# Routing the tokens to experts in two parts, with a fixed region of rows per expert, and the output norm's statistics taken batch by batch

## The chip, the core and the metric

The kernel runs on one core of a Trainium2 chip. The metric is the time of one execution on the device in microseconds, as the median of several executions. TensorE (PE) multiplies and turns matrices, VectorE (DVE) and ScalarE (ACT) work on elements, GpSimd (POOL, here Pool) does elementwise work and issues the indirect transfers, SyncE (SP) issues plain transfers. The engines run side by side and wait for one another through semaphores.

## What is computed

One layer on x of 16 batches x 128 positions x 128 features, in float32. First an attention over each batch, with 16 heads of 64, shared keys and values, one extra null key, a position bias and a causal mask; then a layer norm of its output y; then a mixture of experts on y, whose result is added to x:

```python
def ln(x, g): ...                       # layer norm over the 128 features, gain g, no offset
y = ln(attention(x, ...) @ Wout, g_out)
shared_out = expert(y, sg, su, sd)      # expert: (silu(y @ g.T) * (y @ u.T)) @ d.T, 352 wide
probs = softmax(y @ wr.T + rb)          # 7 routed experts
scores, idx = top_k(probs, 2)
scores = scores / scores.sum(-1)
out = shared_out + sum_e w[e] * expert(y, rg[e], ru[e], rd[e])    # w: the two scores, 0 elsewhere
return x + out
```

Only the two chosen experts need be computed for a token, so the kernel sends each token's y to two of them.

## The kernel before

*Attention.* run_steps runs 19 steps t on every engine (16 batches, three stages deep): in step t TensorE makes the queries of batch t, the scores of batch t - 1, turns P and mixes the values of batch t - 2, and makes the output product of batch t - 3 (project, 16 + 2 matmuls as the trace counts them). Each engine's step is an order written out by hand. VectorE takes each output into y_sb (keep_y). Steps 17 and 18 have only the last batches in them. For batches 0 to 11 the norm of y is spread over these steps: centre_y(0) and scale_y(0) in step 17 on VectorE, with ScalarE's square_y(0) between, gain_y(0) in step 18. Batches 12 to 15 follow after the last step, the same way.

*Routing.* TensorE turns y (12 batches, then 4), ScalarE copies it to YT, and TensorE multiplies by the router's weights; the logits of all 16 batches come together (logits_made). VectorE adds the bias and picks two experts by a chain of small instructions in which each waits for the one before (own). TensorE counts by two products with a strict triangle and a matrix of ones how many rows of each batch go to each expert (ranks_made). VectorE sums these over the batches (run_up), rounds each expert's count up to tiles of 128 rows, sums the tiles (tiles_up) and from them gets each row's place (row_index) in sent_rows, a table in DRAM, in which the experts' tiles lie one behind the other. It then writes the shares, and the table of which expert each of 38 tiles belongs to (tile_expert).

*Tiles.* run_tiles runs 16 shared tiles (one per batch, from YT) and 38 routed ones through a pipeline of four steps: gate and up products (12 matmuls with GH, GL in two precisions), Silu and product, turn, down product. TensorE and VectorE enter it after the table. Pool meanwhile issues 32 indirect transfers, one per batch and choice, each sending 128 rows (y, share, destination) to their places (L485). When all have landed SyncE loads the tiles of rows into a ring of four (L348), each new one when an older is free. The unused rows were filled beforehand by one transfer (L344). Each routed tile's result goes out by an indirect transfer (L491), and at the end all results are loaded and added.

The lines of the profile that recur: L1079 is TensorE's matmul and L1076 its transpose, both in helpers, so tiles tell them apart. L887 and L891 are the scores on VectorE, L623 the exponentials on ScalarE, L761 and L764 the statistics of x, L780 the scaling of x, L732 to L738 the chain of the inverse square root, L864 the gain.

## Time and profile before

| what | us |
|---|---|
| median of 3 runs | 449.41 (448.5 to 451.06) |
| the profiled execution | 449.6 |
| its span in the trace | 447.9 |
| PE busy | 354.8 |
| DVE busy | 285.0 |
| ACT busy | 278.1 |
| POOL busy | 229.6 |

All times in the text are in microseconds from the start of the span. Between the span and the execution's time lie 1.7 us. A busy share is an average over stages: up to some 268 us the attention runs, up to 294 the routing, up to 324 the shared tiles, from 337 to 432 the routed tiles, and the rest adds the results. An idle time in brackets at the end of a row is that of the engine just before the instruction, with the instruction that ended it. A row of a stretch begins with its bounds and length; then come the busy time and the instructions (x) of PE, PE's weight loads, DVE, ACT and POOL, or of DVE alone, then the clock granted to TensorE as a share of 2.4 GHz, the busy share of the DMA engines and GB/s.

### The profile page before, as it was taken

What the parts mean: (1) busy time and instruction counts of PE and PEld (TensorE: products, weight loads), DVE (VectorE), ACT (ScalarE), POOL (GpSimd) and SP (SyncE); (2) the same over time, 40 slices, a digit from 0 to 9 for tenths busy, and PEclk for the clock granted to TensorE, in tenths of its full rate; (3) what the DMA queues carried; (4) which work ended last, traced back from release to release, by engine and by line L of the source; (5) the groups of instructions that cost most, each with busy time, mean ns of one, the idle gap of its engine ahead of it and who ended that gap; (6) DMA issues with size and microseconds to landing.
All of it is one profiled execution on the core that took longest, in us unless ns stands there. A gap on an engine that the chain in (4) does not pass through costs nothing.

```text
span 447.9 us, 10071 instructions
## 1 busy us (share of the span) xinstructions
PE 354.8 (79%) x2917; PEld 296.4 (66%) x2918; DVE 285.0 (64%) x1075; ACT 278.1 (62%) x931; POOL 229.6 (51%) x250
## 2 busy tenths in 40 slices
PE   0286574999999999999999877279908999999940
PEld 0275464677777777777777556279908899998930
DVE  2849246778888888878788886655503555555524
ACT  1384455999999999999999852325503444444410
POOL 5025723777777777777775613067760344444430
PEclk9998886999999999999999996569976999999995
DMA  5716390000000000000000000011111211112108
GB/s 161 243 55 192 106 218 0 2 2 1 1 2 1 3 1 1 3 1 1 2 1 3 2 1 0 0 36 56 51 51 41 56 54 52 48 59 59 41 18 271
DMA packets 29190, 21.28 MB, mean 48 GB/s; under 512 B 4288, under 2 KB 26842, under 8 KB 29150
## 3 DMA queue, kind: packets, MB, share of 16 engines
q1 hardware_dynamic: 23392, 14.23, 12.2%
q0 software_dynamic: 2240, 4.23, 2.7%
q10 hardware_dynamic: 3518, 2.33, 1.8%
q8 instruction: 20, 0.33, 0.3%
q14 instruction: 20, 0.16, 0.1%
HBM read 12.95 MB, written 8.21 MB: 47 GB/s over the span
## 4 chain that ended last, share of the span: by engine, by line
PE 71%; DVE 12%; ACT 6%; DMA 4%; issue 4%; POOL 2%; ACTq 0%; POOLq 0%; DVEq 0%
PE bank L1079 54%; PE bank L1076 16%; POOL sent_rows L485 2%; ACT p_space L623 2%; DMA q_space<-in_L_cond_g_dram 1%; DMA xnT<-result_rows 1%; DVE p_space L887 1%; ACT xn L550 1%; DVE p_space L761 1%; DVE low L891 1%; DVE xn L864 1%; DMA sent_rows<-biasm_space,row_index 1%; DVE stat L738 1%; ACT pT L642 0%; DMA result_rows<-oT_space,dest_ring 0%
## 5 line engine op out<-in xcount | busy, mean ns | idle before, releaser
L454 POOL TENSOR_TENSOR p_space<-p_space,inv 128x516 f32<-128x516 f32 x64 | 66.9, 1046 | 66.5 <-DVE inv L899 66.5
L623 ACT ACTIVATE p_space<-p_space,low 128x129 f32<-128x129 f32 x256 | 98.9, 391 | 1.1 <-DVE low L891 1.1
L887 DVE SCALAR_TENSOR_TENSOR p_space<-bank,rn,biasm_space 128x129 f32<-128x129 f32 x256 | 72.1, 344 | 22.4 <-PE bank L1079 22.2
L445 POOL TENSOR_TENSOR biasm_space<-bias,madd 128x516 f32<-128x516 f32 x64 | 75.4, 1189 | 8.1 <-DVE p_space L887 8.0
L491 POOL DMA_INDIRECT result_rows<-oT_space,dest_ring x38 | 37.3, 983 | 62.3 <-DVE dest_ring L1059 62.3
L696 ACT ACTIVATE biasm_space<-bank 128x384 f32<-128x384 f32 x54 | 26.6, 492 | 56.4 <-PE bank L1076 56.4
L623 ACT ACTIVATION_READ_ACCUMULATOR p_space<-p_space,low 128x1 f32 x256 | 48.3, 189 | 0.0
L1079 PE MATMUL bank<-GH,yh 128*128 (+1 forms) x108 | 41.2, 381 | 7.5 <-DVE yl L1030 7.5
L1079 PE MATMUL bank<-DT,biasm_space 128*128 (+1 forms) x324 | 45.7, 278 | 1.3 <-ACT biasm_space L696 1.3
L1076 PE MATMUL bank<-ident,p_space 128*128 128x128 f32 (+1 forms) x272 | 45.8, 285 | 0.4 <-ACT pT L642 0.4
L891 DVE TENSOR_REDUCE low<-p_space 128x4 f32<-128x516 f32 x64 | 44.2, 691 | 2.2
L1079 PEld LDWEIGHTS bank<-DT,biasm_space 128*128 128x128 f32 x324 | 43.5, 194 | 1.8 <-issue 1.8
L1079 PEld LDWEIGHTS bank<-KB,q_space 64*128 64x128 f32 x512 | 33.6, 194 | 14.6 <-issue 9.2
L1079 PE MATMUL bank<-pT,V 128*64 128x256 f32 x256 | 41.6, 404 | 1.7 <-ACT pT L642 1.3
L1079 PE MATMUL bank<-KB,q_space 64*128 64x129 f32 x512 | 42.9, 298 | 0.0
L642 ACT ACTIVATE pT<-bank 128x512 f32<-128x512 f32 x64 | 37.1, 582 | 6.4 <-PE bank L1079 6.3
L1079 PE MATMUL bank<-xnT,wq_sb 128*128 128x128 f32 x256 | 37.1, 291 | 1.2 <-ACT sq L614 1.2
L1079 PEld LDWEIGHTS bank<-xnT,wq_sb 128*128 128x128 f32 x256 | 32.8, 200 | 6.7 <-issue 5.0
L1030 DVE TENSOR_TENSOR yl<-bank,yh 128x128 fp32r<-128x128 f32 x38 | 11.1, 292 | 40.7 <-ACT yh L707 40.7
L1079 PE MATMUL bank<-GL,yh 128*128 (+1 forms) x108 | 36.2, 335 | 0.0
L1079 PE MATMUL bank<-GH,yl 128*128 (+1 forms) x108 | 36.1, 334 | 0.0
L1076 PE MATMUL bank<-ident,q_space 128*128 128x128 f32 x40 | 12.0, 301 | 30.0 <-DMA q_space<-sent_rows 13.1
(209 smaller groups left out, 708.7 us busy)
## 6 DMA issues: line engine op xcount, KB each, us to landing
sent_rows<-fill_row SPq DMA_DIRECT2D x1, 2470.0 KB, 14.5
q_space<-sent_rows SPq DMA_DIRECT2D x38, 65.0 KB, 1.9
xs<-in_x_dram SPq DMA_DIRECT2D x4, 256.0 KB, 7.0
bias<-bias_rows SPq DMA_DIRECT2D x1, 1024.0 KB, 5.8
xn<-result_rows SPq DMA_DIRECT2D x4, 256.0 KB, 5.2
xnT<-result_rows ACTq DMA_DIRECT2D x4, 256.0 KB, 5.9
out_dram<-xs SPq DMA_DIRECT2D x4, 256.0 KB, 2.4
o_space<-in_L_ffn_rd_dram SPq DMA_DIRECT2D x5, 176.0 KB, 3.0
```

The costliest lines, as they stand in the source:

```text
L445: nc.gpsimd.tensor_tensor(biasm[:, b % 2, heads, :], bias[:, heads, :], madd[:, b:b + 1, :].to_broadcast([P, HC, KEYS]), ALU.add).then_inc ...
L454: nc.gpsimd.tensor_tensor(v, v, spread(inv[:, b % 2, heads], KEYS), ALU.mult).then_inc(p_normed, 1)
L485: nc.gpsimd.indirect_dma_start(out=sent_dram[:, :], out_offset=bass.IndirectOffsetOnAxis(ap=row_index[:, k, b:b + 1], axis=0), in_=send[k] ...
L491: nc.gpsimd.indirect_dma_start(out=result_dram[:, :], out_offset=bass.IndirectOffsetOnAxis(ap=dest_ring[:, m:m + 1], axis=0), in_=result[: ...
L623: last = nc.scalar.activation(v, v, ACT.Exp, bias=low[:, b % 2, h:h + 1], accum_out=den[:, b % 2, h:h + 1])
L642: nc.scalar.activation(pT[:, c % 2, :], bank[turned_bank(t, c)][:, :], ACT.Copy).then_inc(p_kept, 1)
L696: nc.scalar.activation(hT[:, (m - 3) % 2, :], bank[4 + (m - 3) % 2][0:IC, 0:ICH * P], ACT.Copy).then_inc(hT_kept, 1)
L887: last = nc.vector.scalar_tensor_tensor(Pb[:, q, h, :], src, rn[:, q, h:h + 1], biasm[:, q, h, :], ALU.mult, ALU.add)
L891: nc.vector.tensor_reduce(low[:, q, c * HC:(c + 1) * HC], Pb[:, q, c * HC:(c + 1) * HC, :], AX_X, ALU.max, negate=True).then_inc(maxed, 1)
L1030: nc.vector.tensor_tensor(yl[:, m % 2, :], src, yh[:, m % 2, :].bitcast(F32), ALU.subtract).then_inc(yl_made, 1)
L1076: return nc.tensor.transpose(out, in_, ident[0:n, 0:n])
L1079: return nc.tensor.matmul(out, a, b, start=start, stop=stop, skip_group_check=True)
```

## The change

Every expert gets a fixed region of 2,048 rows in sent_rows, so that a row's place needs its expert's number, the count of earlier rows and nothing of the other experts (eoff is added to the first totals). The table grows to 118 tiles, its filling is split over four transfers. Because regions are not adjacent, SyncE reads each tile's first row from a new table, tile_row, four numbers at a time (find_rows). With places independent of later batches, routing runs in two parts: PARTS is batches 0 to 11 and 12 to 15. Part 0 has its logits, choice and count before and around the last output product, its ranks, marks and shares and its 24 sends after; part 1 follows with 8 sends; the table comes last. The send buffers lie elsewhere, part 0's in bias and madd. The norm takes its statistics with bn_stats on each output (keep_y) and bn_aggr; the passes of VectorE over the whole tile and ScalarE's squares go. The constants for counting are made by Pool in step 4. Pool no longer waits for down_kept between the sends.

```diff
+    PARTS = (range(0, Y_FIRST), range(Y_FIRST, NB))
...
+    REGION = NB * S
+    SENT = NE * NB + ROUTED - TOP * NB
+    FILLS = 4
...
+        sent_dram = nc.dram_tensor("sent_rows", (SENT * P, ROW), F32, kind="Internal").ap()
...
+        send = ((rows_in_tile(bias, Y_FIRST), rows_in_tile(madd, Y_FIRST)),
+                (shared(p_space, 0, NB - Y_FIRST, ROW), shared(p_space, (NB - Y_FIRST) * ROW, NB - Y_FIRST, ROW)))
...
-            sp.dma_start(sent_dram.rearrange("(t p) c -> p t c", p=P),
-                         fill_row[:, :].unsqueeze(1).to_broadcast([P, ROUTED, ROW])).then_inc(rows_filled, 16)
-
...
+            for k in range(FILLS):
+                tiles = range(k * SENT // FILLS, (k + 1) * SENT // FILLS)
+                sp.dma_start(sent_dram[tiles.start * P:tiles.stop * P, :].rearrange("(t p) c -> p t c", p=P),
+                             fill_row[:, :].unsqueeze(1).to_broadcast([P, len(tiles), ROW])).then_inc(rows_filled, 16)
...
+            def find_rows(r, n):
+                sp.load(row_regs[0:n], tile_row[0:1, bass.ds(r, n)])
+                return [sp.snap(reg, min_val=0, max_val=(SENT - 1) * P) for reg in row_regs[0:n]]
...
+            sp.wait_ge(table_made, 1)
             sp.wait_ge(rows_sent, 16 * TOP * NB)
...
+            found = find_rows(0, RING)
+            for m in range(RING):
+                load_rows(found[m], m)
...
+                found = find_rows(RING * i + RING, RING)
...
-                    load_rows(RING * i + (RING + m), m)
+                    load_rows(found[m], m)
...
+                if t == 4:
+                    pool.wait_ge(expert_turned, 3 * E)
+                    nc.gpsimd.memset(ones[:, :], 1.0).then_inc(sort_consts, 1)
+                    for k in range(len(PARTS)):
+                        nc.gpsimd.memset(run_up[k][:, :, :, :], 0.0).then_inc(sort_consts, 1)
...
 
...
-                    need(pool, down_kept, min((k * NB + b - 6) // 2, NB - 3))
...
+            pool.wait_ge(rows_filled, 16 * FILLS)
+            for k, batches in enumerate(PARTS):
+                pool.wait_ge(row_index_made, k + 1)
+                for n in range(TOP):
+                    pool.wait_ge(send_made[k][n], 3)
+                    for b in batches:
+                        nc.gpsimd.indirect_dma_start(
+                            out=sent_dram[:, :], out_offset=bass.IndirectOffsetOnAxis(ap=row_index[:, n, b:b + 1], axis=0),
+                            in_=send[k][n][:, b - batches.start, :], in_offset=None).then_inc(rows_sent, 16)
...
-            def square_y(k):
-                b = slice(0, Y_FIRST) if k == 0 else slice(Y_FIRST, NB)
-                act.wait_ge(y_centred, k + 1)
-                nc.scalar.activation(y_squares[:, b, :], y_sb[:, b, :], ACT.Square).then_inc(y_squared, 1)
...
+                if t == NB + 2:
+                    keep_yT(2)
...
-                if t == NB + 1:
-                    square_y(0)
...
+                if t == NB + 1:
+                    keep_yT(0)
+                    keep_yT(1)
...
+            nc.scalar.activation(send[0][1][:, :, 0:D], y_sb[:, 0:Y_FIRST, :], ACT.Copy).then_inc(send_made[0][1], 1)
+            weigh(0)
+            keep_yT(Y_FIRST // 4)
+            for m in range(TOP):
+                nc.scalar.activation(send[1][m][:, :, 0:D], y_sb[:, Y_FIRST:NB, :], ACT.Copy).then_inc(send_made[1][m], 1)
...
+            def scale_y(g):
+                for b in range(4 * g, 4 * g + 4):
+                    last = nc.vector.tensor_scalar(y_sb[:, b, :], y_sb[:, b, :], y_mv[:, b, 0:1], ra[:, b:b + 1], ALU.subtract, ALU.mult)
+                last.then_inc(y_scaled, 1)
+
+            def gain_y(g):
+                dve.wait_ge(y_scaled, g + 1)
+                b = slice(4 * g, 4 * g + 4)
...
+            def norm_y(k):
...
                 dve.wait_ge(y_kept, b.stop)
-                own(nc.vector.tensor_reduce(ma[:, b], y_sb[:, b, :], AX_X, ALU.add))
-                own(nc.vector.tensor_scalar(ma[:, b], ma[:, b], 1.0 / D, None, ALU.mult))
...
-                own(nc.vector.tensor_reduce(va[:, b], y_squares[:, b, :], AX_X, ALU.add))
...
+                for n in PARTS[k]:
+                    last = nc.vector.bn_aggr(y_mv[:, n, :], y_bst[:, n, :])
+                own(last)
+                own(nc.vector.tensor_scalar(va[:, b], y_mv[:, b, 1], EPS, None, ALU.add))
                 own(rsqrt(ra[:, b], va[:, b], ta[:, b], own))
...
+                for g in groups:
+                    scale_y(g)
+                    if g > groups.start:
+                        gain_y(g - 1)
+                gain_y(groups.stop - 1)
...
+            def choose(k):
...
+                dve.wait_ge(logits_made, k + 1)
...
+                nc.vector.tensor_tensor(load[:, b, :], chosen[:, 0, b, :], chosen[:, 1, b, :], ALU.add).then_inc(load_made, 1)
+                nc.vector.tensor_tensor(share[:, 3, b], best[:, 1, b], best[:, 0, b], ALU.subtract).then_inc(gap_made, 1)
...
+            def rank(k):
...
+                base = eoff[:, :] if k == 0 else run_up[0][:, 0, PADS[0] + Y_FIRST - 1, :]
+                nc.vector.tensor_copy(totals[:, b, :], tot)
+                nc.vector.tensor_tensor(up[:, 0, pad, :], tot[:, 0, :], base, ALU.add)
...
+                side, far = 0, 1
...
+                own(nc.vector.tensor_tensor(place[:, b, :], place[:, b, :], up[:, side, pad:pad + n, :], ALU.add))
+                for m in range(TOP):
+                    last = nc.vector.tensor_tensor(placed[:, m, b, :], chosen[:, m, b, :], place[:, b, :], ALU.mult)
...
+                nc.vector.tensor_copy(row_index[:, :, b], row_of[:, :, b]).then_inc(row_index_made, 1)
...
@@ -906,7 +1010,8 @@
                 def keep_y():
                     if on(3):
                         dve.wait_ge(y_made, t - 2)
-                        nc.vector.tensor_copy(y_sb[:, t - 3, :], bank[7][:, 0:D]).then_inc(y_kept, 1)
+                        nc.vector.tensor_copy(y_sb[:, t - 3, :], bank[7][:, 0:D])
+                        nc.vector.bn_stats(y_bst[:, t - 3, :], bank[7][:, 0:D]).then_inc(y_kept, 1)
...
-                if t == NB + 1:
-                    centre_y(0)
...
+                if t == NB + 1:
+                    dve.wait_ge(router_turned, 1)
+                    nc.vector.tensor_copy(router_wT[:, 0:NE], bank[3][:, 0:NE]).then_inc(router_kept, 1)
+                    norm_y(0)
+                if t == NB + 2:
+                    choose(0)
                 keep_y()
...
-                if t == NB + 1:
-                    scale_y(0)
-                if t == NB + 2:
-                    gain_y(0)
...
-            centre_y(1)
-            scale_y(1)
-            gain_y(1)
...
+            for k in range(len(PARTS)):
+                if k > 0:
+                    norm_y(k)
+                    choose(k)
+                mark(k)
+                side = rank(k)
+                share_out(k)
+
+            own(nc.vector.scalar_tensor_tensor(tiles_int[:, 0, :], run_up[1][:, side, PADS[1] + NB - Y_FIRST - 1, :], float(P - 1), eoff[:, :],
+                                               ALU.add, ALU.subtract))
             own(nc.vector.tensor_scalar(tiles_int[:, 1, :], tiles_int[:, 0, :], P.bit_length() - 1, None, ALU.logical_shift_right))
-            nc.vector.tensor_copy(tiles_of[:, :], tiles_int[:, 1, :])
+            nc.vector.tensor_scalar(skipped[:, :], tiles_int[:, 1, :], -float(P), float(REGION), ALU.mult, ALU.add)
...
+            own(nc.vector.tensor_tensor(passed_on[:, :, :], passed[:, :, :],
+                                        skipped[:, 0:NE - 1].unsqueeze(1).to_broadcast([P, ROUTED, NE - 1]), ALU.mult))
+            own(nc.vector.tensor_reduce(tile_skip[:, :], passed_on[:, :, :], AX_X, ALU.add))
+            nc.vector.tensor_scalar(tile_expert[:, RING:RING + ROUTED], tile_float[:, :], 1.0, None, ALU.add)
+            nc.vector.scalar_tensor_tensor(tile_row[:, :], iota_tile[:, :], float(P), tile_skip[:, :], ALU.mult, ALU.add).then_inc(table_made, 1)
...
+            def turn_y(g):
+                pe.wait_ge(y_normed, g + 1)
...
+                pe.wait_ge(p_kept, NCH * (NB - 1) + max(1, g + 1))
+                for b in range(4 * g, 4 * g + 4):
+                    last = turn(bank[y_bank[g]][:, (b % 4) * P:(b % 4 + 1) * P], y_sb[:, b, :])
...
+                if t == NB + 1:
+                    pe.wait_ge(biased, NCH * NB)
+                    turn(bank[3][:, 0:NE], router_sb[:, :]).then_inc(router_turned, 1)
+                if t == NB + 2:
+                    logits(2)
...
+                if t == NB + 1:
+                    turn_y(0)
+                    turn_y(1)
                 mix(2, 2)
+                if t == NB + 1:
+                    turn_y(2)
+                    logits(0)
+                    logits(1)
...
-            for batches in (range(Y_FIRST), range(Y_FIRST, NB)):
-                pe.wait_ge(y_normed, 1 if batches.start == 0 else 2)
-                for b in batches:
-                    last = turn(bank[b // 4][:, (b % 4) * P:(b % 4 + 1) * P], y_sb[:, b, :])
...
+            pe.wait_ge(oT_kept, 2 * NB)
+            count(0)
+            turn_y(3)
+            logits(3)
+            count(1)
...
+                    pe.wait_ge(table_made, 1)
...
-            pe.wait_ge(table_made, 1)
```

TensorE at the end of the attention, from the third-last output product on; `p_space` is P, `pT,V` the mix, `wo_sb` the output product, `xn` is y, `xnT` its turned copy. Before:

```order
L1079 MATMUL bank<-wo_sb,oT_space 128x128 x8
L1079 MATMUL bank<-null_out,pnT 128x128
L1076 MATMUL bank<-ident,p_space 128x128 x4
L1079 MATMUL bank<-pT,V 64x256 x4
L1076 MATMUL bank<-ident,p_space 128x128 x4
L1076 MATMUL bank<-ident,p_space 16x128
L1079 MATMUL bank<-pT,V 64x256 x4
L1079 MATMUL bank<-wo_sb,oT_space 128x128 x8
L1079 MATMUL bank<-null_out,pnT 128x128
L1076 MATMUL bank<-ident,router_sb 128x7
L1076 MATMUL bank<-ident,xn 128x128 x12
L1079 MATMUL bank<-router_wT,xnT 128x7 x12
```

The same engine after, from the last turn of P's null column to the counting (`o_space` holds the load):

```order
L1139 MATMUL bank<-ident,p_space 16x128
L1139 MATMUL bank<-ident,xn 128x128 x8
L1142 MATMUL bank<-pT,V 64x256 x2
L1139 MATMUL bank<-ident,xn 128x128 x4
L1142 MATMUL bank<-router_wT,xnT 128x7 x8
L1142 MATMUL bank<-pT,V 64x256 x2
L1142 MATMUL bank<-router_wT,xnT 128x7 x4
L1142 MATMUL bank<-wo_sb,oT_space 128x128 x8
L1142 MATMUL bank<-null_out,pnT 128x128
L1142 MATMUL bank<-o_space 128x84 x2
L1139 MATMUL bank<-ident,xn 128x128 x4
L1142 MATMUL bank<-router_wT,xnT 128x7 x4
```

The turns of y for batches 0 to 11 and their logits moved ahead of the last output product, among the last two mixes; the count of part 0 moved ahead of the turns of part 1.

VectorE in step 17, from the last exponentials' reciprocals on. Before (centring, then ScalarE's squares, then scaling; `xn` is y, `xnT` the squares):

```order
L850 TENSOR_REDUCE stat<-xn 128x12
L851 TENSOR_SCALAR stat<-stat 128x12
L852 TENSOR_TENSOR xn<-xn,stat 128x1536
L899 RECIPROCAL inv<-den 128x4
L909 COPY xn<-bank 128x128
L857 TENSOR_REDUCE stat<-xnT 128x12
L858 TENSOR_SCALAR stat<-stat 128x12
```

VectorE after, from behind the square root's chain of part 0 to the first instructions of the choice:

```order
L889 TENSOR_SCALAR xn<-xn,stat 128x128 x8
L895 TENSOR_TENSOR xn<-xn,gor 128x512
L889 TENSOR_SCALAR xn<-xn,stat 128x128 x4
L895 TENSOR_TENSOR xn<-xn,gor 128x512 x2
L1013 COPY xn<-bank 128x128
L1014 BN_STATS stat<-bank 128x6
L917 TENSOR_TENSOR o_space<-bank,rbr 128x84
L921 TENSOR_REDUCE best<-o_space 128x12
```

The centring no longer stands ahead of the reciprocal; the whole norm stands behind it and ahead of the copy of batch 14's output, and the choice of part 0 stands ahead of the copy of batch 15's.

## Rows read from the trace of the kernel before

**Rows 1.** TensorE in order of time: start, duration, instructions, idle before with releaser.

```profile
75.57 1.91 PE L1079 MATMUL bank<-xnT,wq_sb 128*128 128x128 f32 x8
...
260.49 0.65 PE L1079 MATMUL bank<-pT,V 128*64 128x256 f32 x4
...
265.68 2.05 PE L1079 MATMUL bank<-wo_sb,oT_space 128*128 128x128 f32 x16 [0.69 <-ACT oT_space L654]
...
277.83 1.11 PE L1076 MATMUL bank<-ident,xn 128*128 128x128 f32 x4 [0.82 <-DVE xn L864]
279.72 1.85 PE L1079 MATMUL bank<-router_wT,xnT 128*128 128x7 f32 x8 [0.78 <-ACT xnT L684]
...
294.32 0.63 PE L1079 MATMUL bank<-GH,yh 128*128 128x352 f32 x1 [7.49 <-DVE yl L1030]
...
323.82 0.49 PE L1076 MATMUL bank<-ident,biasm_space 128*128 128x128 f32 x3
337.43 0.48 PE L1076 MATMUL bank<-ident,q_space 128*128 128x128 f32 x1 [13.12 <-DMA q_space<-sent_rows]
...
344.22 0.27 PE L1076 MATMUL bank<-ident,q_space 128*128 128x128 f32 x1
...
357.94 0.32 PE L1076 MATMUL bank<-ident,q_space 128*128 128x128 f32 x1 [0.53 <-issue]
```

**Rows 2.** Pool in order of time: the first and the last of 32 sends.

```profile
293.72 1.21 POOL L485 DMA_INDIRECT sent_rows<-p_space,row_index  x1 [13.92 <-DVE p_space L1011]
...
333.20 0.96 POOL L485 DMA_INDIRECT sent_rows<-biasm_space,row_index  x1 [0.30 <-issue]
```

**Rows 3.** Chain of waits, behind the last send: start, duration, what.

```profile
333.20 2.31 DMA sent_rows<-biasm_space,row_index
335.53 1.86 DMA q_space<-sent_rows
```

**Rows 4.** Stretches of 2 us: all engines, granted clock, DMA.

```profile
268.00:270.00 2.00, 0.16 (x3) 0.01 (x1) 1.75 (x2) 0.00 (x0) 1.32 (x4) 1.00 0.00 0
272.00:274.00 2.00, 2.00 (x12) 2.00 (x11) 0.70 (x2) 1.16 (x3) 0.00 (x0) 0.50 0.00 0
298.00:300.00 2.00, 2.00 (x14) 2.00 (x13) 0.90 (x3) 1.04 (x3) 1.68 (x2) 0.83 0.20 67
```

**Rows 5.** ScalarE in order of time: the end of the last exponential of batch 15.

```profile
258.81 0.19 ACT L623 ACTIVATION_READ_ACCUMULATOR p_space<-p_space,low 128x1 f32 x1
```

**Rows 6.** VectorE in order of time: statistics, scaling, scores, gain.

```profile
14.45 0.38 DVE L764 BATCH_NORM_AGGREGATE p_space<-p_space 128x2 f32<-128x6 f32 x4
...
21.96 2.14 DVE L780 TENSOR_SCALAR xn<-xs,p_space,stat 128x128 f32<-128x128 f32 x8
...
59.99 1.13 DVE L887 SCALAR_TENSOR_TENSOR p_space<-bank,rn,biasm_space 128x129 f32<-128x129 f32 x4 [3.38 <-PE bank L1079]
...
217.05 1.13 DVE L887 SCALAR_TENSOR_TENSOR p_space<-bank,rn,biasm_space 128x129 f32<-128x129 f32 x4 [0.85 <-PE bank L1079]
...
277.08 0.69 DVE L864 TENSOR_TENSOR xn<-xn,gor 128x512 f32<-128x512 f32 x1
```

**Rows 7.** VectorE by stretch: square root, choice, ranks, tiles, places, table.

```profile
263.88:266.15 2.27, 1.89 (x11) 1.00 0.00 0
281.60:285.60 4.00, 3.58 (x14) 0.50 0.00 0
286.92:289.27 2.35, 2.11 (x8) 0.50 0.00 0
289.27:290.77 1.50, 1.26 (x9) 0.50 0.00 0
290.77:292.17 1.40, 1.30 (x6) 0.50 0.00 0
292.74:293.90 1.16, 1.06 (x7) 0.50 0.00 0
```

**Rows 8.** DMA issues of the page: KB of one, us from issue to landing.

```profile
sent_rows<-fill_row SPq DMA_DIRECT2D x1, 2470.0 KB, 14.5
```

230 lines of the change are left out of this document (110 added, 120 removed).

## Prediction, made before the changed kernel was run

> **What bounds the kernel now.** I read the chain of waits first. It runs through TensorE for the attention (to 268 us), then through VectorE's routing, then TensorE's 16 shared tiles, then Pool's sends, then TensorE's 38 routed tiles. Three places in [rows 1] matter. TensorE starts the first shared tile at 294.32, 26 us after the last attention product; it ends the turning steps of the shared tiles at 323.82 + 0.49 = 324.3; and it then stands 13.12 us until 337.43 for the first routed rows. [rows 2] shows who fills those 13 us: Pool issues 32 sends, the first at 293.72, the last at 333.20, 39.5 us in all or 1.27 each, and they can start only when every row has its place. [rows 3] gives the rest: the last send lands 2.31 us after its start, the row load takes 1.86. So the sends bound the start of the routed tiles, the shared tiles hide 30 us of them. [rows 4] shows what idling costs: TensorE is granted full clock at 268 to 270, half (1.2 GHz) at 272 to 274 after it had stood nearly 2 us, and climbs again between 298 and 300. The reader should see two things: the wait is 13.1 us, and ending it takes either earlier sends or nothing.
>
> **The change, part by part.** Of the 32 sends 24 belong to batches 0 to 11. They now start when part 0 is ranked, not when all is. But the shared tiles start only after part 1's routing and the table, since VectorE runs all of it first. So two dates decide: the first send, and the first shared tile. I follow VectorE and TensorE through the tail.
>
> *Norm of part 0.* VectorE takes it after the last reciprocal of batch 15, which waits for the last exponential, at 258.81 + 0.19 = 259.0 [rows 5]. With the router's copy it starts at 259.3. 12 aggregates at 0.38/4 [rows 6] are 1.1. The chained links cost 2.27/11 = 0.206 each [rows 7], 12 of them 2.5: 262.9. A scale of one batch is 2.14/8, some 0.26 [rows 6]; 8 are 2.0: 264.9; a gain of four batches 0.7, or 0.6 back to back [rows 6]: 265.6 for group 0, 267.2 for group 1, 267.8 for group 2. The whole-tile passes and ScalarE's squares that this replaces cost nothing now on the path but VectorE's own turn.
>
> *TensorE's tail.* Its order is now: turn groups 0 and 1, mix, turn group 2, logits of groups 0 and 1, mix, logits of group 2, and only then the output product of batch 15, which stood at 265.68 before [rows 1]. It idles from 262.5 to 265.6, waiting for group 0; before, an idle of 2 us took the clock away [rows 4], so I take the half level from there. At that level four turns are 1.1 and four batches of logits 1.85 [rows 1]. The output product is 18 matmuls, and 8 of the same shape took 1.91 at half clock [rows 1], so 4.2 (2.5 at full, from the 2.05 and the row after it). A mix is 0.65 at full [rows 1], I take 1.2. Sum: 265.6 + 1.1 = 266.7; group 1 267.2 to 268.3; mix 269.5; turn 270.6; two logits 274.3; mix 275.5; logits 277.3; output product 281.5. So the last attention output comes 13 us later than before. VectorE does choose(0) meanwhile: the 13 links of 112 elements took 4.0 with the gap [rows 7], and between those and the 0.206 of 16 elements I take 3.5 for 84: 280.8, hidden. Count(0) follows the output product, 1.3 (from 285.60, the end of one window of [rows 7], to 286.92, the start of another): 282.9. Rank(0) is the 2.35 plus 1.40 of [rows 7], less one link and smaller: 3.2, so 286.1. Sharing out was the 0.6 between two windows there: 286.8.
>
> *Sends.* Before, the share ended at 292.7 [rows 7] and the first send started at 293.72 [rows 2], 1.0 later. Now 287.8, and 39.5 on, 327.3, the last, if none waits for part 1 (its indices are there at 302, its first send is due at 318). Landed 329.6, loaded 331.5 [rows 3]. The removed waits on down_kept cost nothing: the spacing was 1.27 with them.
>
> *Part 1.* Four aggregates 0.4, 12 links 2.4, 4 scales 1.0, a gain 0.7: 4.6, to 291.4. Turn, copy and logits took 281.60 - 277.70 = 3.9 before (277.83 in [rows 1], the start of choosing in [rows 7]): 295.3. Choosing on 28 elements 2.8: 298.1. Count 1.3: 299.4. Rank with two doublings less, 2.1: 301.5. Sharing 0.6: 302.1. The table was 1.50 + 0.85 [rows 7]; one link goes, a 228-element multiply and reduction come, and the row of each tile: 3.3, 305.4. From the table's end (293.6) to the first shared tile (294.32) it was 0.7: **306.2**, 11.9 later than before.
>
> *Shared tiles and after.* They run 30 us as before, with the same half-clock start: 324.3 + 11.9 = 336.2. The rows are there at 331.5, 4.7 earlier. TensorE goes on at once, 1.2 before 337.43. The two first routed steps took 344.22 - 337.43 = 6.8 at half clock; from 344.22 to 357.94 six took 13.72, or 2.29 each [rows 1]. At full clock 4.6, plus a tenth for the register load that the wait used to hide: 4.7, gain 2.1. Together 3.3.
>
> *What costs nothing.* bn_stats of each output is 0.2 on VectorE, which stands 0.85 before its next group [rows 6]; TensorE is the bound there. Pool's five constants move into step 4, behind its last norm of P, where it next waits for a reciprocal that TensorE's and ScalarE's pace sets; I take nothing, and uncovered they delay one turn of P once, by no more than two sends' length, 2 us. The fill grows from 38 to 118 tiles, 14.5 [rows 8] to about 45 us, from 54 to 100, and nothing waits for it until 287; VectorE's score group took 1.13 inside the old fill and 1.13 long after it [rows 6]. SyncE's register load per four tiles lies in front of waits, with four tiles (9 us) of lead. Its price is not in the trace; TensorE's own costs under 0.8, in the 0.53 of idle at 357.94 [rows 1]. Zero to 0.8, once, and I take zero.
>
> Sum: 449.6 (the profiled execution, 0.2 above the median of three) - 3.3 = **446.3**.
>
> **Rivals.** *The clock holds.* If it falls late or not at all in the tail, the turns, mixes, logits and output product lose about half of their 16 us: choose(0) begins at 272.5, not 277.3, part 1 saves 2 more, the shared tiles start 7 earlier and their slow start (2 us) goes. Then the sends bind: 327.3 - 5 + 4.2 = 326.5, and the time is 446.3 - 9 = 437. For it: the rows hold one fall only, and after it the output product's place is a guess of mine by one idle. Against: that idle was nearly 2 us, this one is 3 and a second of 0.5 follows. In parts, 438 to 443.5. Chance 0.20.
>
> *A longer chain.* I count some forty hand-overs between engines at their best; 3 to 5 us more in them gives 449 to 451.5, level with before. Chance 0.08.
>
> *Slower: sends stretched by VectorE.* 14 sends now fall in 287.8 to 305.4, where VectorE works without pause, not beside tiles. The first old send, which overlapped the table, took 1.21, against 0.96 for the last [rows 2]. At 0.25 more for each of the 14, the last is 3.5 later, under the 4.7 of slack: no change. It decides from 0.34 a send, and the kernel is slower by over 0.5% from (4.7 + 5.6)/14 = 0.74 a send; at 1.0 a send 455.6. Chance 0.06. The Trainium skill (SBUF — State Buffer, "Who interferes with whom") has the rule behind this: copies, casts and tensor_scalar of VectorE in a two-port mode shut GpSimd out of the port that its descriptors are written through. By the page's 3100 ns in place of 620 for a covered send, 14 of them would cost 35 us and, 4.7 of it slack, the time would be about 477; VectorE's instructions of those kinds here are short, some 3 us in all, and no row above shows such a send.
>
> *Slower: the fill.* 30 us of extra writing lie beside steps in which TensorE is never idle; if it slowed them by a fifth, 6 us, the time is 452. Nothing in [rows 6] shows it. Chance 0.05.
>
> **How the numbers follow.** Forecast 0.61, its own range 443.8 to 449; about two thirds of it lie below 447.2, the 0.5% under which a measurement of this kernel can't tell a gain from none. Faster 0.42 + 0.20 = 0.62; same 0.19 + 0.08 = 0.27; slower 0.11. The range takes in the partly held clock and the longer chain: 440.5 to 450.5.
>
> **What would show it.** In the profile after: the output product of batch 15 near 277 with the clock at half (held clock: before 273 at full); the first send near 288, 24 sends without a gap; the first shared tile near 306; no wait between shared and routed tiles, at full clock; row loads waiting for nothing. Wrong would be a gap before the first routed tile (the sends still bind), sends above 1.5 us apart, or attention steps longer than before between 68 and 100 us.

## The result, and the profile after

| | median us | runs | ratio to before, 95% interval |
|---|---|---|---|
| before | 449.63 | 448.50 to 451.06 | |
| after | 446.02 | 444.06 to 447.13 | 0.9911 [0.9884, 0.9937] |

The change makes the kernel 0.9% faster by the ratio, 3.6 us (0.8%) by the medians. The profiled execution took 444.37 (span 442.5), which is 5.2 less than the profiled one of before and 1.7 below the median of after. That difference matters below.

TensorE in order of time, from the last attention steps to the first routed tiles (start, duration, instruction; in brackets the idle time before it and what ended it):

```profile
261.85 0.77 PE L1139 MATMUL bank<-ident,p_space 128*128 128x128 f32 x5
265.80 0.66 PE L1139 MATMUL bank<-ident,xn 128*128 128x128 f32 x4 [3.18 <-DVE xn L895]
267.43 1.11 PE L1139 MATMUL bank<-ident,xn 128*128 128x128 f32 x4 [0.97 <-DVE xn L895]
268.47 1.12 PE L1142 MATMUL bank<-pT,V 128*64 128x256 f32 x4
...
270.43 3.42 PE L1142 MATMUL bank<-router_wT,xnT 128*128 128x7 f32 x16
...
274.83 1.88 PE L1142 MATMUL bank<-router_wT,xnT 128*128 128x7 f32 x8
276.56 3.76 PE L1142 MATMUL bank<-wo_sb,oT_space 128*128 128x128 f32 x16
...
280.71 0.68 PE L1142 MATMUL bank<-o_space 128*128 128x84 f32 x4
289.88 1.12 PE L1139 MATMUL bank<-ident,xn 128*128 128x128 f32 x4 [8.49 <-DVE xn L895]
291.77 1.85 PE L1142 MATMUL bank<-router_wT,xnT 128*128 128x7 f32 x8 [0.78 <-ACT xnT L632]
296.54 1.05 PE L1142 MATMUL bank<-o_space 128*128 128x28 f32 x4 [2.92 <-DVE o_space L929]
304.35 0.63 PE L1142 MATMUL bank<-GH,yh 128*128 128x352 f32 x1 [6.75 <-DVE yl L1093]
...
333.93 0.30 PE L1139 MATMUL bank<-ident,q_space 128*128 128x128 f32 x1
...
338.17 0.27 PE L1139 MATMUL bank<-ident,q_space 128*128 128x128 f32 x1
```

Against [rows 1]: the first shared tile starts at 304.35 in place of 294.32, and the first routed tile at 333.93 in place of 337.43 and with no wait in front of it, where 13.12 stood. Pool in order of time, the first send, one in the middle and the last, against [rows 2]:

```profile
286.18 1.21 POOL L523 DMA_INDIRECT sent_rows<-bias,row_index  x1 [16.58 <-DVE bias L968]
...
304.17 1.07 POOL L523 DMA_INDIRECT sent_rows<-madd,row_index  x1 [0.30 <-issue]
...
325.73 0.96 POOL L523 DMA_INDIRECT sent_rows<-p_space,row_index  x1 [0.30 <-issue]
```

The sends start 7.5 sooner than before and end 7.5 sooner, in front of the last shared tiles. The chain that ended last holds more of VectorE (14%, 12% before) and no longer the sends (POOL had 2% of it); its line by engine on the page:

```profile
PE 72%; DVE 14%; ACT 6%; DMA 3%; issue 3%; ACTq 0%; POOLq 0%; DVEq 0%
```

In stretches of 20 us (busy time of PE, weight loads, DVE, ACT and POOL, then TensorE's granted clock, DMA share, GB/s):

```profile
260.00:280.00 20.00, 15.85 (x79) 12.64 (x79) 10.81 (x48) 5.46 (x9) 2.15 (x2) 0.67 0.00 1
280.00:300.00 20.00, 5.41 (x24) 4.31 (x23) 13.23 (x73) 3.73 (x8) 10.77 (x11) 0.59 0.10 34
300.00:320.00 20.00, 15.65 (x106) 15.66 (x107) 11.48 (x40) 7.50 (x21) 15.12 (x17) 0.81 0.16 55
320.00:340.00 20.00, 19.92 (x153) 19.71 (x152) 11.14 (x36) 10.61 (x30) 5.17 (x6) 1.00 0.14 40
```

In the profile before, these four stretches were granted 0.78, 0.53, 1.00 and 0.73. Both kernels run the end of the routing at half clock. Before, the clock fell a second time, under the 13.12 us wait, and was still at half (0.50 from 337 to 341) for the first routed tile. Now that second fall is gone, but the first one comes earlier and ends later: 0.50 from 268 to 280 and again from 284 to 304, where before it was 0.50 from 272 to 296. It lies on TensorE's own road to the shared tiles, which now holds the turns, the logits and the last output product one behind another.

Two rows of the same view of before, for the comparisons below, the 24 logits of batches 0 to 11 and the counting:

```profile
271.88 5.13 PE L1079 MATMUL bank<-router_wT,xnT 128*128 128x7 f32 x24
...
285.62 1.20 PE L1079 MATMUL bank<-o_space,q_space 128*128 128x112 f32 x4 [4.05 <-DVE o_space L971]
```

### The profile page after: what moved, and what is told of

It reads as the page before. It is cut to its first block, busy times and chain, and to the rows that moved or that the text cites. A ratio compares the mean times of both kernels' runs of the same rounds, so it can differ in the third digit from the quotient of the medians.

```text
span 442.5 us, 10208 instructions
## 1 busy us (share of the span) xinstructions
PE 355.2 (80%) x2921; PEld 295.9 (67%) x2922; DVE 289.0 (65%) x1148; ACT 276.7 (63%) x932; POOL 228.6 (52%) x252
## 4 chain that ended last, share of the span: by engine, by line
PE 72%; DVE 14%; ACT 6%; DMA 3%; issue 3%; ACTq 0%; POOLq 0%; DVEq 0%
PE bank L1142 56%; PE bank L1139 16%; ACT p_space L660 3%; DMA q_space<-in_L_cond_g_dram 2%; DMA xnT<-result_rows 1%; DVE p_space L991 1%; DVE xn L889 1%; ACT xn L588 1%; DVE p_space L806 1%; ACT pT L679 1%; DVE stat L781 1%; DVE low L995 1%; DVE stat L782 1%; DVE stat L783 0%; ACT q_space L642 0%
## 5 line engine op out<-in xcount | busy, mean ns | idle before, releaser
L1142 PE MATMUL bank<-GH,yh 128*128 (+1 forms) x108 | 40.2, 372 | 6.8 <-DVE yl L1093 6.8
L1142 PE MATMUL bank<-pT,V 128*64 128x256 f32 x256 | 42.5, 412 | 0.3 <-ACT oT_space L691 0.2
L1139 PEld LDWEIGHTS bank<-ident,p_space 128*128 128x128 f32 (+1 forms) x272 | 29.5, 140 | 9.3 <-issue 4.0
L1142 PE MATMUL bank<-wo_sb,oT_space 128*128 128x128 f32 x256 | 33.2, 285 | 1.2 <-DVE rn L783 0.7
```

The lines of the kernel that those rows point to most:

```text
L1139: return nc.tensor.transpose(out, in_, ident[0:n, 0:n])
L1142: return nc.tensor.matmul(out, a, b, start=start, stop=stop, skip_group_check=True)
```

## The experiments

Three dates tell nearly everything, so they stand in one table: the first send, the first shared tile, the first routed tile with the wait in front of it, then the rest of the span behind that. The column "at 237" is the start of one and the same output product of the attention, ahead of anything that the change moves. Each row is one profiled execution; the median is that of all timed runs of the kernel.

| kernel | at 237 | first send | first shared | first routed | wait | rest | median |
|---|---|---|---|---|---|---|---|
| before | 236.89 | 293.72 | 294.32 | 337.43 | 13.12 | 110.5 | 449.6 |
| after | 237.22 | 286.18 | 304.35 | 333.93 | none | 108.6 | 446.02 |
| after_again, the same kernel | 237.45 | 287.15 | 305.32 | 335.39 | none | 108.6 | 445.96 (one run) |
| e1 sends held | 237.71 | 301.17 | 304.42 | 345.59 | 11.40 | 110.2 | 457.7 (one run) |
| e2 norm alone | 237.07 | 289.56 | 290.15 | 333.29 | 12.66 | 109.6 | 445.29 |
| e6 split alone | 237.86 | 289.77 | 310.17 | 340.56 | none | 108.5 | 446.57 |
| e10, the same kernel | 236.54 | 287.39 | 307.80 | 337.73 | none | 108.8 | 448.39 (one run) |
| e3 after, early statistics | 237.79 | 285.12 | 303.29 | 332.86 | none | 108.6 | 443.38 |
| e4 after, clock held | 237.65 | 283.58 | 299.84 | 328.17 | 0.33 | 108.8 | 437.95 |
| e5 e3 and e4 | 237.05 | 279.84 | 296.12 | 324.51 | 0.41 | 108.9 | 435.53 |
| e9 after, clock held at the end | 236.32 | 285.99 | 304.27 | 332.55 | none | 108.8 | 443.60 |
| e7 norm alone, clock held | 237.57 | 288.72 | 289.31 | 332.42 | 15.13 | 110.1 | 445.03 |
| e8 split alone, clock held | 237.63 | 286.15 | 306.59 | 334.65 | none | 108.7 | 444.76 |
| e11 before, clock held | 236.50 | 294.33 | 294.93 | 337.99 | 15.10 | 110.3 | 451.20 |

The last part is 108.5 to 108.9 in every kernel that reaches the routed tiles without a long wait, and 109.6 to 110.5 in every one that waits 11 us or more there. So the span ends some 108.7 behind the first routed tile, and one or two later where the clock must first come back; the execution's time is about 1.8 more than the span. Everything below is about that date.

The column "at 237" says how far two traces can be compared. It differs by 1.5 over all rows, and by 1.3 between two executions of one kernel (e6 and e10), which already stand 2.4 apart at the attention's products near 46 us. A difference of about 1 us between the dates of two traces need not come from an edit.

**e1_hold: does the early start of the sends matter at all?** Pool waits for both parts' indices before the first send:

```diff
-                pool.wait_ge(row_index_made, k + 1)
+                pool.wait_ge(row_index_made, len(PARTS))
```

> The changed kernel with one wait moved: part 0's 24 sends also wait until part 1 is ranked (row_index_made 2), as the old kernel's did; regions, tables, fill and norm stay. Theory 1 (the earlier start of part 0's sends carries the gain): first send near 301 instead of 286.2, the last 39.5 later at 340.3, landed and loaded at 344.6, so TensorE stands 10.7 us before the first routed tile and loses its clock again; time 444.4 + 10.7 + 2.1 = 457. Theory 2 (the gain comes from the norm and from routed tiles that run better, the sends are hidden either way): time within 2 us of the changed kernel, 444 to 447.

Measured: 457.7. TensorE in order of time, the first routed tile:

```profile
345.59 0.48 PE L1139 MATMUL bank<-ident,q_space 128*128 128x128 f32 x1 [11.40 <-DMA q_space<-sent_rows]
```

With the sends 15.0 later the wait is back and the first routed tile comes 11.7 later. Within the changed kernel, the early sends are worth about 12 us on the first routed tile, 13 in the time of the profiled execution. That shows that the early start carries the gain, and says nothing yet of what it is worth against the kernel before.

**e2_before_bn: the other half, alone.** The kernel before, with the new norm, and with the gain of part 0 in step 17, where the changed kernel has it, in place of step 18:

```diff
-                        nc.vector.tensor_copy(y_sb[:, t - 3, :], bank[7][:, 0:D]).then_inc(y_kept, 1)
+                        nc.vector.tensor_copy(y_sb[:, t - 3, :], bank[7][:, 0:D])
+                        nc.vector.bn_stats(y_bst[:, t - 3, :], bank[7][:, 0:D]).then_inc(y_kept, 1)
...
-                dve.wait_ge(y_squared, k + 1)
-                own(nc.vector.tensor_reduce(va[:, b], y_squares[:, b, :], AX_X, ALU.add))
+                for n in range(b.start, b.stop):
+                    last = nc.vector.bn_aggr(y_mv[:, n, :], y_bst[:, n, :])
...
-                if t == NB + 2:
+                if t == NB + 1:
                     gain_y(0)
```

> The old kernel with the norm half of the change alone: bn_stats with each output copy, bn_aggr, scaling batch by batch, no passes over the whole tile and no squares on ScalarE; routing, sends and table as of old. The sends bound the old kernel, so each us by which the first send comes earlier is a us of gain. Theory 1 (the norm is worth little alone): part 1 of y is normed 3.8 us earlier, but TensorE's logits of batches 0 to 11 (5.1 us at half clock) then stand in front of it, so the first send is only 2 us earlier: 447.5. Theory 2 (the norm alone brings the whole gain and the split nothing on top of it): first send 4 us earlier, 445.5, level with the changed kernel.

Measured: 445.29, ratio 0.9905 [0.9873, 0.9937]. Theory 1 said 447.5; theory 2, 445.5, was right. The norm alone brings as much as the whole change. What the earlier gain of part 0 has in that was not run by itself. TensorE in order of time:

```profile
264.45 2.05 PE L1066 MATMUL bank<-wo_sb,oT_space 128*128 128x128 f32 x16 [0.69 <-ACT oT_space L650]
...
270.46 2.81 PE L1066 MATMUL bank<-router_wT,xnT 128*128 128x7 f32 x24
274.13 0.66 PE L1063 MATMUL bank<-ident,xn 128*128 128x128 f32 x4 [0.86 <-DVE xn L853]
...
290.15 0.63 PE L1066 MATMUL bank<-GH,yh 128*128 128x352 f32 x1 [7.48 <-DVE yl L1017]
```

Beside [rows 1]: the output product of batch 15 comes 1.2 earlier, since ScalarE has no squares (1.48, at 260.38 before) between its copies, and the turning of part 1, which waits for VectorE's norm, 3.7 earlier (274.13, not 277.83). The first send follows, 4.2 earlier, and the wait behind the shared tiles stays (12.66). The time fell by as much as the first send moved (4.3 and 4.2): in the kernel before, the norm in front of the first send stood on the road to the time. Here TensorE was at full clock for the 24 logits (2.81, not 5.13), but they weren't what the next turn waited for; e11 below shows the same from the other side.

**e6_split_oldnorm and e10_split_again: the split alone.** The changed kernel with the norm of before (centre_y, square_y, and scaling four batches at a time by tensor_tensor):

```diff
-                    last = nc.vector.bn_aggr(y_mv[:, n, :], y_bst[:, n, :])
...
+                dve.wait_ge(y_squared, k + 1)
+                own(nc.vector.tensor_reduce(va[:, b], y_squares[:, b, :], AX_X, ALU.add))
```

> The changed kernel (two parts, fixed regions, table of first rows) with the norm of the kernel before: VectorE sums and centres the rows, ScalarE squares them, VectorE sums the squares and scales four batches at a time. The missing fourth of the square: neither half, the norm alone (445.3), the split alone, both (446.0). Theory 1 (the split alone frees the sends' wait of 13 us but gives most of it back as a later first shared tile; I take the first send at 288 and the first shared tile at 308, four us later than in the changed kernel because part 1's norm is longer too): 448. Theory 2 (the two halves add, the norm is worth 4.3 and the split 0.7 less than nothing): 450.3. A rival reading of the square, that either half alone brings the same 4 us because both move the sends: 445.5.

> The split with the old norm once more, since its profiled execution was the longest of six (451.06, the others down to 445.1). Theory 1 (the first shared tile comes earlier, and the routed steps with it; 109 us follow the first routed step as in every trace here): a run of 445 to 447 with the first routed step at 335 to 337. Theory 2 (the difference lies behind the first routed step): the first routed step at 340.6 again.

Measured: 446.57 in six runs from 445.08 to 451.06, ratio 0.9902 [0.9883, 0.9921], and 448.39 in one more. The third expectation for e6, that either half brings the same four microseconds, is nearest by the median (445.5 against 448); the two traces lie nearer to Theory 1's dates of 288 and 308 (first send 287.39 and 289.77, first shared tile 307.80 and 310.17). The two traces part in front of the first routed tile, not behind it (108.8 and 108.5 follow): half as Theory 1 of e10 had it, though 337.73 is later than the 335 to 337 that I gave. This kernel scatters by 6 us, and only e3 by as much. The traces show from what the 2.4 between their first sends come: 1.3 is there at 237 us already (and still at the last turning of P, 263.96 and 262.64), and the rest is the clock's return. In e10 it came back within the last output product, whose 16 matmuls took 3.50 and the counting behind it 0.65; in e6 they took 3.76 and 1.15.

So the square without a held clock reads, in medians: neither 449.6, norm 445.3, split 446.6, both 446.0. The intervals of the three ratios (0.9905, 0.9902, 0.9911) cover one another. Each half is worth 3 to 4 us, and the second one nothing.

**e3_early: VectorE's chain.** The aggregates and the square root of part 0 go ahead of the last reciprocals of step 17:

```diff
+                if t == NB + 1:
+                    stats_y(0)
                 invert(3, 2)
```

> The changed kernel with part 0's aggregates and square root (3.5 us of VectorE) put ahead of the last reciprocal of step 17, where VectorE stood 2.3 us. Theory 1 (the tail is one chain from part 0's norm over TensorE to the first shared tile): y of group 0 is ready 2.3 us earlier, first shared tile near 302, time 442 against 444.4 of the profiled execution, ratio to the old kernel near 0.984. If the shorter idle of TensorE also keeps its clock, the output product takes 2.5 instead of 4.2 and the time is near 440. Theory 2 (the last reciprocal, 1.2 us later now, takes the gain back through Pool, the turn of P and the last mixes): no change, 446.

Measured: 443.38, ratio 0.9823 [0.9757, 0.9888], 2.6 off the changed kernel's median. The interval is wide because one of the four runs took 438.04, with the highest mean clock of the four (0.928), and the others 443.36 to 443.95; that run was not profiled. The expectation, 442 against the 444.4 of the profiled execution, was too much for the trace: it took 443.41, and all dates come 1.1 sooner. This execution was 0.6 later than the other at 237 us, so the edit itself gave some 1.7 of the 2.3. TensorE in order of time:

```profile
264.72 0.66 PE L1145 MATMUL bank<-ident,xn 128*128 128x128 f32 x4 [1.46 <-DVE xn L895]
266.35 1.11 PE L1145 MATMUL bank<-ident,xn 128*128 128x128 f32 x4 [0.97 <-DVE xn L895]
```

The idle in front of the first turn is 1.46 in place of 3.18, and the clock fell all the same.

**e4_warm: the clock.** TensorE computes products that nobody reads where it would wait: 3 in front of the first turn, 1 behind it, 10 behind the first count, then 1, 3 and 8, each of 384 columns (one of 256).

```diff
+            def warm(*widths):
+                for w in widths:
+                    mm(bank[4][:, P:P + w], ident[:, :], wq_sb[:, 0:w], True, True)
...
+                    pe.wait_ge(pn_kept, NB)
+                    warm(*[384, 384, 384])
                     turn_y(0)
+                    warm(*[384])
                     turn_y(1)
...
             count(0)
+            warm(*[384, 384, 384, 384, 384, 384, 384, 384, 384, 384])
```

> The changed kernel with products added that nothing reads (26 of 256 or 384 columns into a free PSUM bank), placed where TensorE waits between the last turn of P and the first shared tile, so that it never idles long. Theory 1 (half clock costs the tail some 5 us and the shared tiles' start 2): clock full from 260 to 330, choice of part 0 at 274 instead of 276.75, first shared tile near 299, last send near 322.5, first routed tile near 327, time 437.5. Theory 2 (the added products run past the waits and push the turns back, or the clock does not stay up): 444 to 450.

Measured: 437.95, ratio 0.9730 [0.9712, 0.9748], as Theory 1 had it. TensorE in order of time:

```profile
263.76 2.20 PE L1142 MATMUL bank<-wq_sb,ident 128*128 128x384 f32 x6 [0.73 <-ACT pnT L672]
266.21 0.66 PE L1139 MATMUL bank<-ident,xn 128*128 128x128 f32 x4 [0.24 <-DVE xn L895]
...
269.50 1.85 PE L1142 MATMUL bank<-router_wT,xnT 128*128 128x7 f32 x16
...
271.86 1.51 PE L1142 MATMUL bank<-router_wT,xnT 128*128 128x7 f32 x8
273.22 3.76 PE L1142 MATMUL bank<-wo_sb,oT_space 128*128 128x128 f32 x16
...
288.71 1.03 PE L1142 MATMUL bank<-router_wT,xnT 128*128 128x7 f32 x8 [0.34 <-ACT xnT L632]
...
299.84 0.40 PE L1142 MATMUL bank<-GH,yh 128*128 128x352 f32 x1 [1.31 <-DVE yl L1093]
...
328.17 0.33 PE L1139 MATMUL bank<-ident,q_space 128*128 128x128 f32 x1 [0.33 <-DMA q_space<-sent_rows]
```

The turns of part 0 take 0.66, where after has 1.11 from the second on, sixteen logits 1.85 in place of 3.42, the first shared tile comes 4.5 sooner and the shared tiles need 28.3 in place of 29.6. The last row shows that the sends now bind again, by a third of a microsecond: both roads to the first routed tile are about equally long. The clock was not held throughout: the output product of batch 15 ran at half here too (3.76).

**e9_warm_tail: which of these products counts.** Only the last eight are left:

```diff
             count(1)
+            warm(*[384, 384, 384, 384, 384, 384, 384, 384])
```

> The changed kernel with the last eight of the unread products alone, those behind part 1's counting, right ahead of the first shared tile. Nothing is left out. Theory 1 (they bring only the part of the gain that lies in the shared tiles themselves, which start at half clock: in the trace of the changed kernel the first shared tile to the first routed step takes 29.6, with all the products 28.3, and part of the 6.7 us wait may become busy work at half clock that ends a little late): 444.7 against 446.0. Theory 2 (the clock ahead of the shared tiles is what matters for all that follows, the routed steps too): 440.

Measured: 443.60 (443.24 to 444.15), ratio 0.9877 [0.9846, 0.9908]. In the trace the first shared tile stands where it stood (304.27) and the shared tiles take 28.3, 1.3 less, as Theory 1 had it. This execution was 0.9 earlier at 237 us and had the late clock of after_again below: from there to the first shared tile it took 67.95, after_again 67.87 and after 67.13, so the eight products moved nothing ahead of it. 2.4 against the median of after is more than that, but the two intervals overlap, and in after_again the shared tiles took 30.1, 1.8 more than with the added products. Theory 2 falls: the larger part of e4's gain, over 5 us, is made ahead of the shared tiles.

**e7_before_bn_warm and e8_split_oldnorm_warm: each half with the clock held.** Products like those of e4, in e2 (3, 1, 1, 6 and 11 of them) and in e6 (6, 1, 13, 1, 3, 8). The diff is two of the places in e7:

```diff
             turn(bank[4][:, 0:NE], router_sb[:, :]).then_inc(router_turned, 1)
+            warm(3)
...
             last.then_inc(logits_made, 1)
+            warm(6)
```

> The kernel before with the new norm alone (445.3 so far), and unread products in TensorE's waits: three behind the router's turning, one between the two parts, one ahead of the last logits, six behind them, eleven behind the counting. Nothing is left out. Against the changed kernel with such products (437.95) it shows what the split is worth once the clock is held. Theory 1 (here the sends end last and the products can only shorten the road to the first send, from 289.56 to some 287.5): 443, so the split is worth 5 us with a held clock and nothing without. Theory 2 (the gain from the products is a gain of clock alone, the same in both kernels): 437.5, and the split is worth nothing either way.

> The split with the old norm, and unread products in TensorE's waits (six ahead of part 0's turning, thirteen behind its counting, then one, three and eight). Nothing is left out. It shows what the norm is worth when the clock is held, against 437.95 with both halves. Theory 1 (with the clock held every us of VectorE's chain ahead of the table is on the path, twice: the norm of part 0 and that of part 1; from the two first sends, 289.8 against 286.2, and the longer norm of part 1): 442.5, the norm is worth 4.5. Theory 2 (the halves overlap here as they do without the products, 446.6 against 446.0): 438.5.

Measured: e7 445.03 (444.25 to 445.22), ratio 0.9893 [0.9876, 0.9909]; e8 444.76 (443.25 to 445.25), ratio 0.9888 [0.9852, 0.9923]. TensorE in e7 in order of time:

```profile
270.94 2.81 PE L1066 MATMUL bank<-router_wT,xnT 128*128 128x7 f32 x24
...
276.04 1.03 PE L1066 MATMUL bank<-router_wT,xnT 128*128 128x7 f32 x8
```

Its first routed tile, in the same view:

```profile
332.42 0.47 PE L1063 MATMUL bank<-ident,q_space 128*128 128x128 f32 x1 [15.13 <-DMA q_space<-sent_rows]
```

With the norm alone a held clock gives 0.3: it makes the wait for the sends longer (15.13) and little else. Theory 1 for e7 had the mechanism but 2 us too much for it. With both halves such products gave 8.1 (e4), with the split alone 1.8. Held, the square reads: norm alone 445.0, split alone 444.8, both 438.0. So the split is worth some 7 us on top of the norm once the clock is held, and nothing if it isn't. The norm's 6.8 on top of the split is an upper bound, since e8 carries two costs of its own. The six products ahead of the first turn ran past the date at which VectorE had group 0 ready (268.78), so the turn started at 270.89. And the clock was not held for part 1: its eight logits took 1.85, as at half clock, behind a wait of 2.30.

**e11_before_warm: the fourth corner.** The kernel before with the products of e7.

```diff
             last.then_inc(logits_made, 1)
+            warm(6)
```

> The kernel before with the same unread products (three behind the router's turning, one between the parts, one ahead of the last logits, six behind them, eleven behind the counting), neither half of the change. Nothing is left out. It is the last corner of the square with the clock held: norm alone 445.0, split alone 444.8, both 438.0. Theory 1 (in the kernel before every us ahead of the first send counts, and the products give back half a clock there: 24 logits in 2.8 instead of 5.1, four turnings and eight logits 1.3 sooner, the counting 0.5 sooner; 4.1 in all, of which the longer wait ahead of the first routed step takes 0.3): 446. Then in the kernel before most of what the norm alone brought (4.3) was clock, and the held-clock gains are 1, 1.2 and 8 us: the halves are worth their gain only together. Theory 2 (the products bring as little here as with the norm alone, 0.3): 449.6; the held-clock gains are 4.6, 4.8 and 11.6, near a plain sum.

Measured: 451.20 (449.73 to 452.70), ratio 1.0034 [1.0019, 1.0049]: slower, and both theories fall. TensorE in order of time:

```profile
271.30 2.81 PE L1079 MATMUL bank<-router_wT,xnT 128*128 128x7 f32 x24
273.98 1.04 PE L1079 MATMUL bank<-wq_sb,ident 128*128 128x384 f32 x2
277.25 1.11 PE L1076 MATMUL bank<-ident,xn 128*128 128x128 f32 x4 [2.23 <-DVE xn L864]
...
281.00 6.01 PE L1079 MATMUL bank<-wq_sb,ident 128*128 128x384 f32 x12
286.85 0.59 PE L1079 MATMUL bank<-o_space,q_space 128*128 128x112 f32 x4
```

The 24 logits are 2.3 faster and it helps nobody: the next turn waits for VectorE's old norm of part 1 until 277.25, and before it was 277.83 (in an execution that was 0.4 later at 237 us). Here VectorE sets the date, not the clock. Then the six products run at half clock, end at 287.0 instead of some 285, and the counting behind them starts at 286.85, where the same view of before has 285.62. With the 0.4 at 237 us the first send is 1.0 later than in before; the profiled execution (450.12) is one of the fastest of the ten, and what makes the median 1.5 higher than before's beyond this 1.0 is open. So this corner holds a cost of its own, and no sum over the square is drawn from it.

**e5_both: the best of them.** e3 and e4 in one kernel, with fewer products around the first turn than e4 has, against which this diff is:

```diff
-                    warm(*[384, 384, 384])
-                    turn_y(0)
                     warm(*[384])
+                    turn_y(0)
+                    warm(*[256])
                     turn_y(1)
```

> The changed kernel with both edits of the two runs before: the aggregates and the square root of part 0 are put ahead of the last reciprocals, and TensorE computes unread products (the identity by the query weights, into bank 4) where it would wait. Nothing is left out. Theory 1 (with the clock held the sends are what ends last, so an earlier date is worth what it moves the first send, and no more): the first send comes some 1.1 us before the 283.58 of the run with the products alone, and the time is 436.8. Theory 2 (the two edits add in full to the changed kernel's 446.0): 446.0 - 2.6 - 8.1 = 435.3.

Measured: 435.53 (435.04 to 435.75), ratio 0.9679 [0.9663, 0.9696], 3.2% faster than before and 2.4% faster than the change as made. The sum, 435.3, met the median and Theory 1, 436.8, did not. Theory 1 took the first send to move by 1.1; it moved by 3.7 between the two traces. The first turn of y stands 2.2 sooner (263.98, not 266.21): 0.6 of it is there at 237 us, the rest is the early statistics. Behind it the clock stayed full to the end of part 0:

```profile
269.62 1.06 PE L1148 MATMUL bank<-router_wT,xnT 128*128 128x7 f32 x8
270.53 2.03 PE L1148 MATMUL bank<-wo_sb,oT_space 128*128 128x128 f32 x16
```

where e4 needed 1.51 and 3.76 for the same. What it said of the end holds: the first routed tile moved as the first send did, 3.7 sooner both, and the profiled execution with them (435.34, not 438.96). By the medians it is 2.4, since the traced execution of e4 is the slowest of its four. That the sum met the median is therefore in part luck: it adds two gains, and in the trace a third thing, the clock behind the first turn, belongs to neither alone.

**after_again: a second trace of the changed kernel.**

> The changed kernel once more. Its runs lie in two groups, about 444.2 with a mean granted clock of 0.925 and about 446.4 with 0.908. Both theories expect one of the two; if it falls in the second, the trace shows in which stretch the clock is lower.

Measured: 445.96, with a mean granted clock of 0.906; the six runs of after have 0.925 twice (444.37 and 444.06) and 0.907 to 0.910 four times (445.88 to 447.13). TensorE in order of time:

```profile
276.79 3.76 PE L1142 MATMUL bank<-wo_sb,oT_space 128*128 128x128 f32 x16
...
281.20 1.15 PE L1142 MATMUL bank<-o_space 128*128 128x84 f32 x4
290.84 1.11 PE L1139 MATMUL bank<-ident,xn 128*128 128x128 f32 x4 [8.49 <-DVE xn L895]
...
305.32 0.63 PE L1142 MATMUL bank<-GH,yh 128*128 128x352 f32 x1 [6.77 <-DVE yl L1093]
```

In the first trace the clock was back at full when the counting ran (0.68); here it was not (1.15). The next turn is 0.96 later, the first shared tile 0.97, the first routed one 1.46 (335.39), the span 1.5. Of the 0.97 at the first shared tile 0.23 is there at 237 us already. The other 0.5 of the span lies in the shared tiles, 30.1 in place of 29.6. So the profiled execution lies below the median with a clock that came back in time for the counting; that the four runs of the lower clock are like after_again is read from their mean clock alone, since they weren't traced.

## Why the prediction was right, and where it wasn't

The forecast was 446.3 and the median is 446.02, inside the forecast's own range. The mechanism was right for the kernel with both parts; the credit that the prediction gave to each part was not. The steps, with what the profiled execution shows:

- **VectorE's norm of part 0** (start 259.3, group 0 normed at 265.6): 259.5 and 265.7. Links of 0.205 where I took 0.206. Right.
- **TensorE's tail at half clock**: right from the second turn on (1.11), the first still ran at full (0.66). Logits ended at 276.7, forecast 277.3; the output product at 280.8, forecast 281.5, since 16 matmuls took 3.76 and the last two 0.5. The prediction had placed all this by one idle of 3 us. The clock fell there in every trace of the split without added products, but behind idles of 3.2, of 4.3 (e6, e10) and of 1.46 (e3); in e2, with an idle of 2.1, it stayed full for the 24 logits behind it (2.81). So the length of the idle doesn't tell, and that the fall came where it was forecast is in part luck.
- **Counting part 0**, 1.3 from the output product's end to the first step of the ranks: the term that was mis-sized. It was 0.7 here (280.8 to 281.49), the counting's matmuls taking 0.68 because the clock had come back; 1.15 in the other trace. This 0.6 and the 0.7 of the output product make most of the 1.6 by which the first send (286.18) was earlier than forecast (287.8). The execution of after_again, where the counting took 1.15, is 1.6 longer, and that is most of what the forecast lay above the profiled one (446.3 and 444.37). The sum met the median to 0.3; against the profiled execution it was 1.9 too high, and which of the two groups of runs the median falls in was nothing that the sum could know.
- **Sends**: 39.55 from first to last, forecast 39.5. None waited for part 1.
- **Part 1 and the table**: from the first share (forecast 286.8, measured 285.3) to the table's end I counted 18.6; measured 303.85 - 285.27 = 18.6. The first shared tile came 10.0 later than before, forecast 11.9, and 1.5 of that difference is the earlier start of this chain.
- **Shared tiles**: 29.6, forecast 30. The first routed tile comes 3.5 sooner (forecast 1.2), the two first routed steps take 4.2 (forecast 4.7, before 6.8), and all behind the first routed tile is 1.9 shorter (forecast 2.1).
- **What cost nothing**: bn_stats put 2.5 us more on VectorE between 100 and 240 us (117.1 busy in place of 114.6), while TensorE was busy 140.00 of 140 in both. The filling ran to some 97 us, and at 237 us the changed kernel was 0.3 later than before, well inside the scatter of one kernel. TensorE's register load shows as an issue gap of 0.31 at 342.79 (0.53 in [rows 1]); SyncE's loads held no tile, since no routed tile of this trace waits for its rows. Right, as far as that scatter lets one see.

**What failed** is one sentence: that the passes and squares which the new norm replaces "cost nothing now on the path but VectorE's own turn". They stood on the path in the kernel before, and e2 puts 4.3 us on them (with the earlier gain of part 0), more than the whole sum of 3.3. The prediction worked out the dates of the combined kernel correctly and gave the credit to the split, without asking what the norm would do alone. The forecast held only because the two gains don't add: the split takes the shared tiles 14.2 later than e2 has them (304.35 and 290.15) to free a wait of 12.66, and TensorE does that stretch at half clock.

**The rivals.** *The clock holds* (437) did not come of itself; made to hold, it gave 437.95, so its price was right, and the sends bind again there (0.33), as it said. *A longer chain*: no; part 1 had its hand-overs as counted. *Sends stretched by VectorE*: in the changed kernel none was. 14 sends start beside VectorE's chain there, 0.95 to 1.01 long behind the first (1.21, as before), and 1.26 to 1.32 apart. The Trainium skill (SBUF — State Buffer, "Who interferes with whom") names copies, casts and tensor_scalar in a two-port mode as what can block them. Its 3100 ns in place of 620 beside a copy, in the page's section "A bandwidth-pool intuition that's wrong (but worth ruling out)", would be five times as long. No send here shows that; the one at 288.95, which starts beside four tensor_scalar of 128x128 (287.98 to 289.09), took 0.97. But with the old norm two sends in 32 were longer by 0.5 each. Pool and VectorE in e6 in order of time:

```profile
289.77 1.69 POOL L525 DMA_INDIRECT sent_rows<-bias,row_index  x1 [17.32 <-DVE bias L982]
...
294.28 1.47 POOL L525 DMA_INDIRECT sent_rows<-bias,row_index  x1 [0.31 <-issue]
```

```profile
289.69 0.69 DVE L912 TENSOR_TENSOR xn<-xn,stat 128x512 f32<-128x512 f32 x1
...
294.23 0.69 DVE L899 TENSOR_TENSOR xn<-xn,stat 128x512 f32<-128x512 f32 x1
```

In e6, e8 and e10 alike these two sends start 0.05 to 0.08 behind such an instruction over 512 columns; in the changed kernel one of the same size starts 0.18 behind a send (289.13 and 288.95), and that send took 0.97. The longer sends cost nothing, since no routed tile waits for its rows in those kernels. *The fill*: no cost can be seen; the 0.3 at 237 us is inside the scatter.

## What to carry to other kernels

Before a change of two parts is credited, work out each part alone against the bound of the kernel before: here either half gave the same 3 to 4 us, and the second one nothing more, since what it freed went into a longer road through TensorE at half clock. Where work is moved so that TensorE's chain of small products becomes the road to the bound, count what its waits do to the clock; products that nobody reads, put where the engine waits anyway, were worth 8 us in such a kernel, 0.3 where another engine's queue bound, and cost 1.5 (1.0 of it traced) where they stood in front of work that was due. Two traces are to be set against each other from a point that the edit can't reach. And compare a sum with the median only after looking at how the execution that was profiled stands to it.
